# Four places for eight units of the maxima in each of the first stage's last nine chunks, and a new order for the attention

## What is computed

```python
def reference(x, wq, bq, wk, bk, wv, bv, wo, bo, Wr, br, W1, b1, W2, b2):   # x: 4 x 2048 x 256, float32
    x = x + layernorm(attention(layernorm(x), ...))       # 16 heads of 16, causal, softmax over 2048 keys
    x = x + layernorm(experts(layernorm(x), ...))         # two of eight experts per batch, exact gelu
    return x
```

## Time and profile before

| | |
|---|---|
| median of 3 runs | 1991.49 us (1989.31 to 1994.93) |
| the profiled execution | 1991.74 us, of which its span 1990.0 us |
| PE busy over the span | 1950.9 us, 98% |
| DVE busy | 1784.6 us, 90% |
| ACT busy | 1365.3 us, 69% |
| POOL busy | 295.6 us, 15% |

### The profile page before, as it was taken

One profiled execution on the slowest core, in us unless ns is written; L12 is line 12 of the kernel. 1 busy time (PEld: TensorE's weight loads), 2 busy tenths in 40 slices (PEclk: granted clock), 3 DMA queues, 4 the chain that ended last, 5 costly groups with the idle time before them and its releaser, 6 DMA issues. The chain is left out here.

```text
span 1990.0 us, 39435 instructions
## 1 busy us (share of the span) xinstructions
PE 1950.9 (98%) x15684; PEld 854.6 (43%) x15684; DVE 1784.6 (90%) x3574; ACT 1365.3 (69%) x1655; POOL 295.6 (15%) x358
## 2 busy tenths in 40 slices
PE   9999999999999999999999999999999998999998
PEld 6655333333333333333333333333333343667665
DVE  7876999999999999999999999999999985799984
ACT  5766757777777777777777777777777767333432
POOL 4333101011111111010111111110101211322100
PEclk9999999999999999999999999999999999999999
DMA  6877606040404124250504041232506213344321
GB/s 180 255 220 209 136 11 123 16 93 9 92 23 85 44 55 68 35 88 11 93 9 92 16 91 42 58 61 42 92 7 136 82 38 119 85 127 124 96 69 43
DMA packets 151706, 162.93 MB, mean 82 GB/s; under 512 B 58466, under 2 KB 124386, under 8 KB 151522
## 3 DMA queue, kind: packets, MB, share of 16 engines
q1 hardware_dynamic: 146658, 151.98, 32.7%
q0 software_dynamic: 4864, 8.44, 1.9%
HBM read 100.03 MB, written 60.29 MB: 81 GB/s over the span
## 5 line engine op out<-in xcount | busy, mean ns | idle before, releaser
L628 DVE TENSOR_REDUCE b_pmax<-b_ring 128x1 f32<-128x512 f32 (+4 forms) x2282 | 1329.0, 647 | 62.3 <-PE b_ring L618 51.1
L1339 ACT ACTIVATE b_prob<-b_psS 128x1024 f32<-128x1024 f32 (+3 forms) x1280 | 1084.8, 895 | 359.3 <-PE b_psS L1382 353.9
L1382 PE MATMUL b_psS<-g_qT,g_kT 33*128 33x512 bf16 (+7 forms) x5120 | 832.8, 348 | 9.8 <-ACT b_prob L1339 7.7
L618 PE MATMUL b_ring<-g_kT,g_qT 64*128 64x512 bf16 (+3 forms) x2498 | 712.1, 348 | 3.9 <-DVE b_pmax L628 2.1
L1399 PE MATMUL b_psO<-b_prob,g_v 128*32 128x512 f32 (+3 forms) x5120 | 595.5, 540 | 0.4 <-ACT b_outT L1349 0.3
L1382 PEld LDWEIGHTS b_psS<-g_qT,g_kT 64*128 64x128 bf16 (+1 forms) x5120 | 295.6, 94 | 462.7 <-ACT b_prob L1339 349.4
L1309 POOL TENSOR_SCALAR_AFFINE_SELECT b_prob<-b_prob 128x512 f32<-128x512 f32 x256 | 163.4, 638 | 1296.6 <-ACT b_prob L1339 1296.3
L618 PEld LDWEIGHTS b_ring<-g_kT,g_qT 64*128 64x128 bf16 x2498 | 220.5, 94 | 251.4 <-DVE b_pmax L628 177.7
L616 PE MATMUL b_ring<-later,query_of 64*128 64x128 bf16 x988 | 190.6, 219 | 2.0 <-DVE b_pmax L628 1.5
L1399 PEld LDWEIGHTS b_psO<-b_prob,g_v 128*32 128x32 f32 x5120 | 103.2, 108 | 168.0 <-issue 133.5
L1753 PE MATMUL c_psH<-c_yT,c_w1e 128*128 128x512 f32 x256 | 116.7, 604 | 10.4 <-ACT c_hT L1674 7.5
(11 more groups left out here) (162 smaller groups left out, 1055.9 us busy)
## 6 DMA issues: line engine op xcount, KB each, us to landing
qk_parts<-a_parts SPq DMA_DIRECT2D x64, 384.0 KB, 4.5
g_qT<-qk_parts SPq DMA_DIRECT2D x184, 128.0 KB, 4.5
g_kT<-qk_parts SPq DMA_DIRECT2D x184, 128.0 KB, 5.0
out_sums<-b_outT SPq DMA_DIRECT2D x64, 256.0 KB, 2.9
v_ones<-a_v SPq DMA_DIRECT2D x16, 544.0 KB, 5.8
g_v<-v_ones SPq DMA_DIRECT2D x32, 272.0 KB, 4.9
a_x<-in_L_attn_x SPq DMA_DIRECT2D x16, 512.0 KB, 4.9
c_x<-in_L_attn_x SPq DMA_DIRECT2D x15, 512.0 KB, 5.0
```

The source lines that it names most:

```text
L618: ins_ = self.nc.tensor.matmul(to, groups.qT[own, g, h // 2, 0, t * P:(t + 1) * P], groups.kT[own, g, h // 2, 0, pc * CH:pc * CH + w], sta ...
L628: self.nc.vector.tensor_reduce(pmax[:, c % 2].rearrange("p (h t) n -> p h t n", t=TT)[:, heads[0]:heads[-1] + 1:2, qt, pc], bank[:, 0:k * ...
L1339: nc.scalar.activation(prob[:, j % PBUF, 2 * s:2 * s + 2, off:CH], psS[:, 2 * s:2 * s + 2, off:CH], ACT.Exp).then_inc(exp_done, 1)
L1382: ins_ = nc.tensor.matmul(psS[:, 2 * s + p, off:CH], kT[own, g, s, ab, kt * P:(kt + 1) * P], qT[own, g, s, ab, c * CH + off:(c + 1) * CH], ...
```

## The change

`LEAD_TIMES` goes from 3 to 4, so that 72 units are done in the first stage and 2264 in the attention. The places are now: 0 as before, 1 between q and k's second half and the turn, 2 in the middle of v, 3 behind v. `ORDERS` is written anew throughout, and the rest of the first stage's last chunk stands at other steps. Of the eight strings the first line is shown.

```diff
-REST_MIDDLE_AT = 26
-REST_LOW_AT = 30
+REST_MIDDLE_AT = 24
+REST_LOW_AT = 25
 REST_STORED_AT = 34
...
 LEAD_FROM = 7
-LEAD_TIMES = 3
+LEAD_TIMES = 4
 LEAD = 2 * LEAD_TIMES * (B * NC - LEAD_FROM)
...
 ORDERS = (
-    "a101a1010b0ab1010aa0101b1010av1a110bb0001v01ab010101b0101bv0b011a101aav0b0b011bbvb0101a1010bav1a1aa1010b"
+    "0b011ab01a010a110aa010a1vba1010b0011v0101b0011b0101a1010bv01ab01vb0101a1010bbvb0101a101ab0v0b0b0101bav1a"
...
@@ stage_a, block.vector @@
                 if chain:
                     normalise(chain, n + 2)
                 lead(n, 2)
+                lead(n, 3)
...
@@ stage_a, block.tensor @@
                     if i == 1:
                         lead(n, 0)
+                lead(n, 1)
                 if n == BIAS_AT + 1:
                     sum_bias()
                 if n + 1 < N:
                     turn(n + 1)
-                lead(n, 1)
                 if n > 0:
                     pe.wait_ge(v_copied, n)
                 for t in range(TT):
                     for k in range(KD):
                         ins_ = nc.tensor.matmul(psV[:, t], xT[:, n % 2, k, t * P:(t + 1) * P], w[:, 2, k],
                                                 start=(k == 0), stop=(k == KD - 1))
+                    if t == TT // 2 - 1:
+                        lead(n, 2)
                 ins_.then_inc(v_done, 1)
-                lead(n, 2)
+                lead(n, 3)
```

More of the change, by code:

```diff
@@ L434 @@
[L434 to L449, removed]
@@ new lines @@
+    "v01011a10b00101abvva1010ba1010bva1010b01a10bva1010b0101abv1a10b01a10b0va1010b0101aava1010b01a10v0bb1a010"
+    "ba101v1aa0b010b011abv1a10b00101aaa0101b1010v01010b011bb01010b01a1va1010b010b1avb0101aa1010av0ba10101a10b"
+    "vb0101ab0101ava1010b010ba1vb0101a1a100bv0b01010ba1va1a11av0b0b0101bava1010b0101abva1010b0b01a1vb0101a101"
+    "0bavb0101a1010bavab01010bv1a10ba1vb0010101abv10100b011b0101a10b01v1a10b0v",
+    "a1b0010101avb0a1110100v1010b0101a1010abv0b01a1vb0101ab0101avb0101a1a10b0vb0101a1010bava10b010101abvba101"
@@ new lines @@
+    "ba11v0101a1010ba1010bvva1010ba1010bva1010b01a10bvb0101ab0101ava1010ba1010bva1010b0b01a1va1010a101a0a1010"
+    "v0b1a010b1aa0ba1v1a100b1a10b0v1ab010b00v1a1b001a1v10101010aa10101a10b0v1a100bav1a10b00101abv1a0b01010ba1"
+    "va1010b0101abv0b1a1010b01avb0101a1010bava1010b0101bava1010b0101abva1010b0101abvb01010b01a1avb0101ab0101a"
+    "va1010b0101abvb0101a1010bava110101abv0b0010ba1v10101a100a01010b01a1vba1010v",
+    "0ba101010b1va110b0001a1v10100ba1010101bavvb01010ba101avb0101a1010bavb0101a100ba1vb0101ab0101avb001a1101b"
@@ new lines @@
+    "101a0v0101a1010ba1010bvvb0101ab0101av0b011a1a100bva1010ba1010bvb0101a1010bavb0101a10b01av0ba1010101abv1a"
+    "010b1a010bbabv1a0b01a10b10b110b0bv0ba1101010bav0101ab0101v1a1100100ba1010bva1010bb010a1v0b011aa1010bva10"
+    "10ba1010bv1a0b010b01a1va1010b0101abvb0101a1a100bv0b01a10101abva1010b0b011ava10101a10b0bva1010ba1010bvb01"
+    "01ab0101ava1010ba1010bva1b0010bv1a101a1b00va110b0a1100v10101a100b0101bav0101bav",
+    "0b0101a110va1b001a1100va11100010aa1010bv01a10bv1a100b0b01a1ava1010b0101abva1010b0101abvb0101a1010bavb001"
@@ new lines @@
+    "001111bb1010101ab0vva1010ba1010bva1010b0101abvb0101a10b01ava1010b0101abvb0101a1010bava1010b0101abvba1010"
+    "1010bbbv1aab010ba0110a0101aa10b0a010va1101a1b0v1010ba1010a10101a010bvb0101ab0101av01a10bv1a100b0101bava1"
+    "010ba1010bvb0101a101a0bva1010b01a10bv10b010bav1a10b0b0v1a1a1010abvb0101a1010bavb0101a1010bava1010b0101ab"
+    "va1010b0101abvb0101a1010bavab01010b0va11a110b0v1010101a0a1010101ab0va110b0v",
+    "0ba1010101ava110b00011v0101ab0101b0101avva101010b01abva1010ba1010bva1010ba1010bvb0101a1010bavb001a11010a"
@@ new lines @@
+    "a110b1010101avb0101ab0vv1a10b010b01ava1010b01a10bvb0101ab0101ava10101ab010bva1010b0101abva1010b0b01a1vba"
+    "1010b0b01a1v1aa0b010b101abb0101bvab01010101av10100ba11b01010a1010bv1010ab0101av010b1a10b0va1010ba1v0b1ab"
+    "10101a0v0b01101a10bav1a100ba1010bva1010b0101abvb0101a1010abvb0101a10b01avb0101a1a10b0va10b010101abvb0101"
+    "ab0101avb0101ab0101ava11010ba1vb0010b0a1v10101a100aa1010101a0bvb001a1a1010v1a1b00v",
+    "1a110b0001va11100010ba01a1v0ba1010bvvb01a101010bav1a1a010ba1v0b0b0101abva1010b0101abvba1010101ab0vab0101"
@@ new lines @@
+    "110101b0101avvb0101a10b01avb0101a1010bavb0101a1010bav0b01a1010ba1vb0101a1010bbvb0101a10b0b1v1aa1a10b00b0"
+    "1v0bb1a101a0b01av0b01a111b00bb1010a0101v0101a1100aa10101a10b0vb0101a100ba1va1010bb0101bv1a10b01010bava10"
+    "10ba1010bvb0101a101ab0va1010b0101abv1a1010bavb010b0b0v1a101a1a0bvb01001a101abvb0101a1010bava1010b0101abv"
+    "a1010b0bv1a101a10b0vab0101a11v0b0a110b0v10101a100a01011a10b0va110b0v",
+    "1a1001a1b00vab0101001a1v10100ba1010101bavvb0101ab0101avb0101ab0101avb0101a0b01a1vb0101a1010bavb0011ba101"
```

111 lines of the change are left out of this document (48 added, 63 removed).

## The result

The changed kernel takes 1976.42 us (median of 4 runs, 1973.57 to 1979.87), the kernel before 1991.38 (4 runs); the ratio is 0.9924 with an interval from 0.9902 to 0.9945, so 15 us less. The profiled execution took 1975.9 us, its span 1974.2.

A forecast was written before the change was run, and what follows sets the result against it. PE was taken to bound the first stage and DVE, narrowly ahead of PE, the attention with maxima. Terms 4.7 - 10.7 - 3 - 3 + 1 = -11.0 us against 1991.7 gave 1980.7, stated as 1980.5 us; own range 1975 to 1986.

The forecast's parts named there:

- Term 2: Attention, first group's third chunk: 18 units fewer take 10.7 us off DVE, gained in full where DVE binds; lower bound 2.9.
- Term 3: Attention, first group's end: the stall from 27 units piled ahead of v of steps 21 to 24 goes, -3 us, bounds 0 and about 7.
- Term 5: Last chunk's rest: `low` one step behind ACT's cast, so DVE may wait for it, +1 us, bounds 0 and 1.9.
- Term 4: Attention up to step 616: fewer same-half neighbours and more units right ahead of v, -3 us, bounds 0 and 10.
- the wider one: Whole kernel: the range for 8 in 10, from 1973 to 1991 us.
- Term 1: First stage's last nine chunks: nine more places for units at 0.53 us each on PE, +4.7 us, lower bound 2.9.
- The third rival: First stage, places around v's last half: DVE can't keep up, 21 us lost, kernel 2002 us; chance 5%.
- the second rival: Attention: PE binds, so the units save 2.9 us and cost 4.7, kernel 1993.5 us; chance 8%.
- The new order stalls somewhere else: Place left open: stretches at half clock or less of DVE's time used give back 3 to 14 us, 1984 to 1995 us; 7%.
- SP's queue does the same transfers: SP's DMA queue: no placing of shifts moves into the first stage beyond the two there; no time given.
- PE binds: Attention: PE sets the time, units save 2.9 us and cost 4.7, kernel 1993.5 us; chance 8%.
- the order is no better: Attention: the new order gains nothing, only the units' saving and the first stage's cost hold, 1985.7 us; chance 12%.

The follow-up runs named there:

- front_later: Changed kernel with the last stage's first contexts loaded from step 580 on, not 576; 1968.54 us, ratio 0.9893 to the kernel before.
- v_uncut: Changed kernel with the contexts' loads at step 580 and the third place behind v's second half, so v is not cut; 1981.38 us, ratio 0.9944 to the kernel before.
- old_order_even: Changed kernel's four places with the old order, 18 unit signs taken out evenly between the products with v of steps 1 and 20; 1993.94 us, 1.0020 to before.
- old_order_pile: Changed kernel's four places with the old order, 18 unit signs taken out ahead of the products with v of steps 21 to 24; 1996.43 us, 1.0023 to before.
- new_start: Changed kernel with its new order up to the product with v of step 101, then the old signs; 1980.02 us, ratio 0.9952 to the kernel before.
- stock_more: Changed kernel, contexts' loads at step 580, one unit moved from behind v to ahead of it at 74 places in steps 80 to 560; 1995.46 us, 1.0016 to before.
- stock_spoiled: Changed kernel, contexts' loads at step 580, one unit moved from ahead of v to behind it at 96 places in steps 80 to 560; 2005.27 us, 1.0064 to before.

## Why the prediction was right, and where its steps failed

**The total** was right, but terms of it stand for other mechanisms than I gave, and errors cancel: the first 40 steps gained 3 us more than terms 2, 3 and 5 (15.7, not 12.7), the later ones 9.6 more than term 4 (12.6, not 3), and a stall that I had only as a rival took 6.8 back. Without that stall, in front_later, the kernel takes 1968.5 us, below the forecast's own range and the wider one, so that the total came out right is in part luck.

**Term 1** (+4.7) was right: +4.5 us, with PE busy for 118.82 of 119 us and no wait of PE for `b_pmax`. v_uncut shows that the place of the cut matters: two places in a row would have cost 10.6 us more than the cut does. The third rival, DVE too late in the first stage, didn't come: DVE waits 0.96 us there for PE. (Two times inside that rival are 0.1 us off: 163.1 + 1.29 is 164.4, and 1.38 more is 165.8; its end, 167.05, is right.)

**Term 2** (-10.7, "gained in full where DVE binds") failed in its condition. In the new order the 18 units are worth 12.9 us at the place where I put them back, a little more than the term; in the old order 0.3 to 4.1. The step that failed is "in full": from the waits of the whole attention I concluded that DVE bound the first 40 steps by 10.7 us and more. It did bind up to step 22 (57.49 of 58.16 us), but with PE's own work close behind (shown busy for 53.96 of 56.07 us in old_order_even), so that 10.1 us less for DVE shortened that part by 2.1. That is the second rival's mechanism, PE binding, in this one stretch of the old order. What the new order does otherwise is to use the time: it keeps 93 units ahead of step 22 and takes 20 of the 45 out of steps 22 to 30. Of the 23 units fewer in the first 40 steps, 6 are done in the next 40, which take 0.2 us more.

**Term 3** (-3, the pile-up) named the right place but only one of its causes, and the size was off. From step 22 to 30 the old order takes 31.8 us and the new one 17.5, so 14.3 us. Thinning the pile-up alone left 28.7. Two other causes are shown one at a time in the new order: scores that stand 1.2 steps ahead of v in place of 3.0 and 2.2 cost 6.3 us, and the rest at steps 26 and 30 costs 3.2 us up to step 30 and 4.8 up to step 40. The 20 units fewer are left for the remainder of 5 us, to which the 3.1 us of old_order_pile (13 fewer) fit; that was not tried apart in the new order. These shares hold only in this order of taking them: with all 45 units in place DVE's own 28 us would have stood against any other cure, and with the scores 1.0 step ahead, fewer units gave 3.1 us. The half clock near 270 was little of its price: with the clock at 1.00 throughout, old_order_even still takes 29.8 us there. I had counted in the order "48 signs, where it was 31" between the last unit and the first score, and had not counted how far the scores then are ahead of v, which was in the same strings: 1.0 step in the old order.

**Term 4** (-3, bounds 0 to 10) was too small and its reasons fell: steps 40 to 560 are 12.6 us shorter, beyond the bound. new_start shows that it is the signs there. That fewer same-half neighbours among the scores bring it is refuted (150 more of them: 0.2 us), and so is that more units right ahead of v help as such. What goes with the time in all four orders is how evenly the units lie: the units beyond four in one step, summed over steps 80 to 560, are 63 in the new order, 100 in the old (+13 us), 97 in stock_more (+27) and 121 in stock_spoiled (+37). The sign is right each time, the size per unit differs by a factor of two and more, so this is a correlation with a mechanism that is seen in single steps (2.49 and 3.08 us), and the cause of the 12.6 us is not shown. Of the profile's signs, DVE's idle time came out as forecast (51.6 us, below 62), and PE's waits for DVE did not: they grew from 177.7 to 317.4 us.

**Term 5** (+1, bounds 0 to 1.9) had the wrong sign. DVE doesn't wait for the cast (269.87 is where the reduction ahead ends), and putting the rest at these steps is worth 4.8 us in this order. I had written that the new order keeps a step free of units beside it and took nothing for it.

**The rivals.** "The new order stalls somewhere else" came true beside the forecast: a wait of 4.25 us, 6.8 us in all. "SP's queue does the same transfers" was the sentence that failed: the transfers are the same, but the chunk's `place` moved behind one more context's loads, and I had counted signs on PE and DVE and not on SP's queue at the last iteration. "PE binds" fell with the order's gain; "the order is no better" too.

## What to carry to other kernels

- A saving on an engine that binds is worth only what the next limit behind it leaves: here 2.1 us of 10.1 in a stretch where PE was nearly as busy. Count per stretch the load of every engine and how far each producer runs ahead of its consumer (here the scores ahead of v).
- With a ring of three banks, work handed from one in-order engine to another must lie evenly: in the steps looked at, one unit too many cost up to a whole reduction, and the step that lost it gave 0 to 0.22 us back, in whichever direction it moved.
- When an order moves, look at every queue it passes. A transfer of a few KB on the critical path that is issued behind bulk loads waits for them; moving the bulk loads four steps was worth 7 us, about half as much as the whole change.
